# Bucket tiles of four heads stacked by transfers, and the maximum taken by four exponentials in every unit

## The reference

```python
q = split_heads(hidden_states @ Wq + bq)          # 16 heads of 8 features
k = split_heads(hidden_states @ Wk + bk)
scores = jnp.einsum('bhqd,bhkd->bhqk', q, k) / scale
pos_k = (rel_embeddings @ Wk + bk)                # 64 buckets of relative position
c2p_att = jnp.einsum('bhqd,hpd->bhqp', q, pos_k)
c2p = jnp.take_along_axis(c2p_att, c2p_pos, axis=-1)
p2c_att = jnp.einsum('bhkd,hpd->bhkp', k, pos_k)
p2c = jnp.swapaxes(jnp.take_along_axis(p2c_att, p2c_pos, axis=-1), -1, -2)
probs = jax.nn.softmax(scores + (c2p + p2c) / scale, axis=-1)
out = einsum('bhqk,bhkd->bhqd', probs, v) @ Wo + bo + hidden_states
out = layernorm(out, 1e-7) * ln_scale + ln_bias   # a second, plain layer norm follows
```

## Time and profile before

| what | value |
|---|---|
| median of 3 executions | 2843.77 us (2837.84 to 2845.44) |
| the profiled execution's own time | 2838.59 us |
| its span (first to last instruction) | 2836.9 us |
| busy in the span: TensorE, VectorE, ScalarE, GpSimd | 85%, 79%, 81%, 25% |
| mean granted TensorE clock | 0.939 of full |

### The profile page before, as it was taken

How to read it: one execution, slowest core, us unless ns; L and a number is a source line. 1 busy time by engine, 2 the same in 40 slices (tenths; PEclk the granted TensorE clock), 3 DMA queues, 4 the chain that set the end, 5 groups by cost and what they waited for, 6 DMA issues and landing times. The chain is left out here.

```text
span 2836.9 us, 64292 instructions
## 1 busy us (share of the span) xinstructions
PE 2414.7 (85%) x18180; PEld 1323.1 (47%) x18199; DVE 2232.0 (79%) x6591; ACT 2286.8 (81%) x4255; POOL 711.7 (25%) x565
## 2 busy tenths in 40 slices
PE   2888888888888337746699999999999999999997
PEld 1555555555555226614344444444444444444443
DVE  3788888788888576785488888888888888888887
ACT  1888888888888353317699999999999999999997
POOL 2334534544444101124311111111111111111114
PEclk7899999999999659977799999999999999999999
DMA  2000000000000100000011111211111121111113
GB/s 78 13 22 12 11 17 16 11 13 20 11 11 12 44 0 1 0 30 0 16 45 53 52 45 45 60 45 45 52 52 45 45 60 45 45 53 51 45 45 89
DMA packets 182540, 96.04 MB, mean 34 GB/s; under 512 B 22539, under 2 KB 179291, under 8 KB 182491
## 3 DMA queue, kind: packets, MB, share of 16 engines
q1 hardware_dynamic: 182491, 95.45, 12.0%
HBM read 78.10 MB, written 4.73 MB: 29 GB/s over the span
## 5 line engine op out<-in xcount | busy, mean ns | idle before, releaser
L1955 DVE TENSOR_TENSOR c_Hl<-c_HF,c_Hh 128x512 f16<-128x512 f32 x1028 | 679.6, 688 | 160.9 <-ACT c_Hh L1842 144.7
L1838 ACT ACTIVATE c_HF<-c_H,c_b 128x512 f32<-128x512 f32 x1028 | 711.0, 692 | 64.2 <-PE c_H L1777 44.3
L1842 ACT ACTIVATE c_Hh<-c_H,c_b 128x512 f16<-128x512 f32 x1028 | 706.4, 687 | 0.0
L1893 POOL TENSOR_TENSOR c_EX<-c_euler,c_D 128x16 f32<-128x16 f32 x65 | 188.6, 2902 | 1194.6 <-DVE c_D L1928 1194.6
L1775 PE MATMUL c_H<-c_Ch,SH 128*128 128x512 f16 x1028 | 390.1, 379 | 0.0
L1777 PE MATMUL c_H<-c_Ch,SH 128*128 128x512 f16 x1028 | 390.0, 379 | 0.0
L1776 PE MATMUL c_H<-c_Cl,SH 128*128 128x512 f16 x1028 | 390.0, 379 | 0.0
L1786 PE MATMUL c_Y<-c_Hh,SH 128*128 128x512 f16 x1024 | 388.1, 379 | 0.3 <-DVE c_Hl L1955 0.3
L1788 PE MATMUL c_Y<-c_Hl,SH 128*128 128x512 f16 x1024 | 388.1, 379 | 0.0
L1787 PE MATMUL c_Y<-c_Hh,SH 128*128 128x512 f16 x1024 | 388.1, 379 | 0.0
L692 DVE CUSTOM_DVE_ANT_0 a_T<-a_S,a_POS 128x128 f32<-128x128 f32 x1024 | 234.8, 285 | 48.0 <-PE a_S L436 41.0
(11 more groups left out here) (300 smaller groups left out, 4372.8 us busy)
## 6 DMA issues: line engine op xcount, KB each, us to landing
c_CWB<-c_rows SPq DMA_DIRECT2D x260, 256.0 KB, 4.1
a_QN<-a_QH SPq DMA_DIRECT2D x128, 32.0 KB, 1.9
a_KN<-a_KH SPq DMA_DIRECT2D x128, 32.0 KB, 1.8
out<-d_O SPq DMA_DIRECT2D x16, 256.0 KB, 2.3
a_QN<-a_QL SPq DMA_DIRECT2D x64, 32.0 KB, 1.9
a_KN<-a_KL SPq DMA_DIRECT2D x64, 32.0 KB, 1.8
CUR<-in_ctx SPq DMA_DIRECT2D x1, 1848.0 KB
c_rows<-c_CWR SPq DMA_DIRECT2D x65, 8.0 KB, 1.4
```

Source lines behind the costliest of these rows:

```text
L1838: act.activation(HF[:, k % 4, :], bH[k % 4][:, :], ACT.Gelu_apprx_tanh, bias=b1[:, g % EXPERTS, f:f + 1], scale=1.0 / WSCALE).then_inc(hf_ ...
L1842: act.activation(Hh[:, g % 2, f, :], bH[k % 4][:, :], ACT.Gelu_apprx_tanh, bias=b1[:, g % EXPERTS, f:f + 1], scale=1.0 / WSCALE).then_inc( ...
L1955: dve.tensor_tensor(Hl[:, g % 2, f, :], HF[:, k % 4, :], Hh[:, g % 2, f, :], ALU.subtract)\
```

## The change

- **Bucket tiles.** A tile now holds four heads in one copy (`TILES` 8). ScalarE writes the f16 high part without a scale to the new `ST`, VectorE the low part, and SyncE puts both into `AB` with 16 transfers of 128 KB a block (`stack_rows`), eight after the last query tile and eight after the last key tile. One tile a step, in steps 5 to 12. The first chunk waits for all 16. ScalarE's first write of each kind waits for the transfers of the block before.
- **Maximum.** `EARLY_MAX` is empty: `take_max` goes, and every unit has four exponentials.
- **Order.** The projections of queries, keys and values go to steps 1, 2 and 10 to 13; `high_half` goes behind the exponentials of steps 1 and 2, `low_half` to steps 2 and 3, `values_in` to 14. The last layer-norm step goes from step 9 to 14 and is written with a broadcast tensor in place of a second scalar. `QN` and `KN` have one semaphore a group.
- **Preparation.** The engines begin when the weights are in, and x comes in three transfers: the first four sequences, the next four, and the other 56 behind the small late loads. GpSimd's large fills come after its first copy. The table is half as wide, and VectorE's steps on it have half as many instructions.
- **TensorE.** Four 128x512 matmuls that nobody reads end the tail, ahead of the next block's scores. `V` has 16 columns a head, not 32.

```diff
-TILES = 4 * NG
+TILES = 2 * NG
-NORM_STEPS = (2, 3, 4, 5, 6, 7, 9)
+NORM_STEPS = (2, 3, 4, 5, 6, 7, 14)
+TILE_STEPS = (5, 6, 7, 8, 9, 10, 11, 12)
+V_STEPS = (10, 11, 12, 13)
-EARLY_MAX = range(6, 14)
-VCOLS = 32
+EARLY_MAX = range(0, 0)
+VCOLS, TILE = 16, 32
...
-        HM = sb("HM", [P, 2, TOK], F16)
-        AB = sb("AB", [P, S, 2, NG, 2, NB], F16)
+        ST = sb("ST", [P, 2, 2, S, NG, NB], F16)
+        AB = sb("AB", [P, 2, 2, S, NG * NB], F16)
...
+            def stack_rows(i, nxt, kind):
+                hold(sp, spare_sp, ab_ok.sem, ab_ok.at(i, TILES * nxt + (kind + 1) * NG))
+                if nxt:
+                    hold(sp, spare_sp, g_ps.sem, g_ps.at(i, CHUNKS))
+                for h in range(HG):
+                    for low in range(2):
+                        at = 64 * (h // 2) + 32 * low
+                        sp.dma_start(AB[at:at + 32, kind, h % 2, :, :].rearrange("p s x -> p (s x)"),
+                                     ST[32 * h:32 * h + 32, kind, low, :, :, :].rearrange("p s g b -> p (s g b)"))\
+                            .then_inc(ab_in[kind].sem, 16)
...
-                for src, dst in loads + late:
+                for src, dst in loads:
                     sp.dma_start(dst, src).then_inc(loaded, 16)
+                for n in range(2):
+                    sp.dma_start(X[:, n * NB:(n + 1) * NB, :], tokens[:, n * NB:(n + 1) * NB, :]).then_inc(x_in, 16)
+                    if n == 0:
+                        sp.wait_ge(x_in, 16)
+                for src, dst in late:
+                    sp.dma_start(dst, src).then_inc(late_in, 16)
             def body(i):
                 stack_queries(i, 1)
                 stack_keys(i, 1)
+                for kind in range(2):
+                    stack_rows(i, 1, kind)
...
             def position_chunk(i, nxt, c):
                 if c == 0:
-                    pe.wait_ge(ab_ok.sem, ab_ok.at(i, TILES * (1 + nxt)))
+                    for done in ab_in:
+                        pe.wait_ge(done.sem, done.at(i, done.per * (1 + nxt)))
...
-                                         AB[64 * f:64 * f + 64, at, :, :, :, :], start=True, stop=True)
+                                         AB[64 * f:64 * f + 64, :, :, at, :], start=True, stop=True)
...
+                    if u == UNITS + TAIL - 1 and not last:
+                        for _ in range(4):
+                            pe.matmul(bO[:, :], window[:, 0:P], table[:, 0:2, :, :].rearrange("p g k n -> p (g k n)"),
+                                      start=True, stop=True)
...
             def high_rows(i, nxt, n):
                 act.wait_ge(a_ps.sem, a_ps.at(i, TILES * nxt + n + 1))
-                act.wait_ge(ab_ok.sem, ab_ok.at(i, TILES * nxt + n - 1))
-                act.activation(HM[:, n % 2, :], bG[n % 2][:, :], ACT.Copy, scale=low_rows[:, :]).then_inc(hm_ok.sem, 1)
+                kind, g = n // NG, n % NG
+                if g == 0 and nxt:
+                    act.wait_ge(ab_in[kind].sem, ab_in[kind].at(i, ab_in[kind].per))
+                act.activation(ST[:, kind, 0, :, g, :], bG[n % 2][:, :].rearrange("p (s b) -> p s b", b=NB),
+                               ACT.Copy).then_inc(hm_ok.sem, 1)
...
             def split_rows(i, nxt, n):
-                dve.tensor_tensor(AB[:, :, kind, g, j, :], bG[n % 2][:, :].rearrange("p (s b) -> p s b", b=NB),
-                                  HM[:, n % 2, :].rearrange("p (s b) -> p s b", b=NB), ALU.subtract)\
-                    .then_inc(ab_ok.sem, 1)
+                dve.tensor_tensor(ST[:, kind, 1, :, g, :], bG[n % 2][:, :].rearrange("p (s b) -> p s b", b=NB),
+                                  ST[:, kind, 0, :, g, :], ALU.subtract).then_inc(ab_ok.sem, 1)
...
-                    last = dve.tensor_scalar(X[:, bass.ds(i * NB + b, 1), :], R[:, b, :], mv[:, b, 0:1],
-                                             rstd[:, b:b + 1], ALU.subtract, ALU.mult)
+                    last = dve.scalar_tensor_tensor(
+                        X[:, bass.ds(i * NB + b, 1), :].rearrange("p a h -> p (a h)"), R[:, b, :], mv[:, b, 0:1],
+                        rstd[:, b:b + 1].to_broadcast([P, H]), ALU.subtract, ALU.mult)
```

More of the change, by code:

```diff
@@ L58, in by_dve, with tiles_of @@
     return sum(1 for k, f in DVE_CHUNKS if k <= c)
+def tiles_of(u):
+    return [n for n, step in enumerate(TILE_STEPS) if step == u]
 def row_x(kind, g, j, b):
-    return ((kind * NG + g) * 2 + j) * NB + b
+    return ((kind * 2 + j) * NG + g) * NB + b
 class Count:
@@ L268, in body @@
                 stack_keys(i, 1)
+                for kind in range(2):
+                    stack_rows(i, 1, kind)
             stack_queries(0, 0)
             stack_keys(0, 0)
+            for kind in range(2):
+                stack_rows(0, 0, kind)
             body(0)
@@ L356, in body @@
             def body(i, first=False, last=False):
+                if first:
+                    pool.wait_ge(x_in, 32)
+                    pool.wait_ge(late_in, LATE)
                 if not last:
                     copy_block(i, 1)
-                if not first:
-                    power(i - 1, 0)
                 for u in range(UNITS):
@@ L363, in body @@
                         take_max(i, u)
-                    if u == NORM_STEPS[5] and not first:
-                        power(i - 1, 1)
-                residuals(i)
+                    if u in (NORM_STEPS[1], NORM_STEPS[5]) and not first:
+                        power(i - 1, (NORM_STEPS[1], NORM_STEPS[5]).index(u))
+                residuals(i, first)
                 if not last:
@@ L500, in _ @@
             pe.wait_ge(tab, 5)
-            project_qk(0, 0)
-            project_v(0, 0)
+            project_q(0, 0)
+            project_k()
+            for b in range(NB):
+                project_v(b)
             pe.wait_ge(tab, TAB)
@@ L527, in body @@
                     if u == 1 and not last:
-                        project_qk(i, 1)
+                        project_q(i, 1)
                     if u == 2 and not last:
-                        project_v(i, 1)
-                    for n in range(2 * (u - 6), 2 * (u - 6) + 2):
-                        if 0 <= n < TILES and not last:
+                        project_k()
+                    if u in V_STEPS and not last:
+                        project_v(V_STEPS.index(u))
+                    for n in tiles_of(u):
+                        if not last:
                             bucket_tile(i, 1, n)
@@ L861, in body @@
                             softmax_outputs(i, b)
-                    if u == 1 and not last:
-                        low_half(i, 1, 0)
-                        low_half(i, 1, 1)
-                    if u == 2 and not last:
+                    if u in (2, 3) and not last:
+                        low_half(i, 1, u - 2)
+                    if u == 14 and not last:
                         values_in(i, 1)
@@ L868, in body @@
                         norm_step(i - 1, NORM_STEPS.index(u))
-                    for k in range(2 * (u - 6), 2 * (u - 6) + 2):
-                        if 0 <= k < TILES and not last:
+                    for k in tiles_of(u):
+                        if not last:
                             split_rows(i, 1, k)
```

146 lines of the change are left out of this document (75 added, 71 removed).

## The result

The changed kernel takes 2735.16 us (median of 4 runs, 2734.89 to 2737.46), the kernel before 2844.47 beside it (2837.84 to 2845.44): a ratio of 0.9622, interval 0.9606 to 0.9639, or 109 us less. The profiled execution took 2735.33, with a span of 2733.6. The forecast of 2733 is 2 us off.

The account below looks back on a forecast made before the run. The prediction took ScalarE and its waits as the bound, then the transfers. Blocks (91.5 us) and preparation (19.5) off the profiled 2838.6 gave 2727.6; with 5.2 for the median, 2733, its own range 2708 to 2758.

Parts of the forecast that it names:

- The block: Attention block: head 35.8 us, ended by the transfers, plus tail 12.8 make 48.6 for 54.7, a gain of 6.1.
- a sign of being wrong: Head of the block: SyncE's queue, now with 40 transfers a block, would itself be what ends the head.
- rival 2: ScalarE's ST copies are written at xT's slow rate: 4.0 us a block, 60 in all, 2793 us; chance 0.07.
- Rival 3: Stacking transfers are slower than the queue issues them: 2.4 us a block, 2774 us in all; chance 0.08.
- The first reading of the profile: Steps with bucket tiles, before: ScalarE busy 20.55 of 22.60 us and VectorE less, so ScalarE is the engine to count.
- ScalarE's sum: Head: ScalarE's operations add to 33.9 us after the change and 34.0 before, so only waits can be won.
- ScalarE's waits: Head: 0.6 us of VectorE's 1.8 stays and step 14 costs 0.3, so ScalarE's head is 34.8.
- GpSimd's 2.6 go with `take_max`: Head: ScalarE's waits for GpSimd's subtraction, 2.6 us a block, vanish when the subtraction is removed.
- The preparation: Before the first chunk: start 15.9 us earlier, table work 4.1 less, first chunk at 53.2 for 72.70, 19.5 won.
- Rival 4: GpSimd holds up the norm step in step 14: 2.1 us a block for 0.3, 2760 us in all; chance 0.10.
- Rival 5: Transfers make the kernel slower: from 1.55 us each the whole gain is gone, at 2.0 it takes 2898; chance 0.04.
- Rival 1: Half the head's waits stay, 4 us instead of 0.9: a block wins 3.0, 2779 us in all; chance 0.12.

Follow-up runs that it names:

- e10: Changed kernel with each of a block's last eight stacking transfers cut into two of half the bytes: 2837.82 us, ratio 0.9986 to before.
- e4: Changed kernel with the last norm step moved back from step 14 to step 9, in its new form: 2740.72 us, ratio 0.9652 to before.
- e2: Kernel before with GpSimd's subtraction taken out (`EARLY_MAX` empty) and nothing else: 2844.19 us, ratio 1.0011 to before.
- e5: Changed kernel with GpSimd's subtraction back in units 6 to 13 and the last norm step in step 9: 2758.27 us, ratio 0.9713 to before.
- e11: Changed kernel with its bucket tiles two a step, in steps 5, 7, 9 and 11: 2752.48 us, ratio 0.9684 to before.
- e7: Changed kernel with TensorE, ScalarE and VectorE waiting at their start for all loads again: 2758.47 us, ratio 0.9715 to before.
- e1: Changed kernel with GpSimd's subtraction back in units 6 to 13, last norm step still in step 14: 2837.63 us, ratio 0.9985 to before.
- e6: Changed kernel with GpSimd's subtraction back and the last norm step in step 14 in its old form: 2837.66 us, ratio 0.9988 to before.
- e3: Changed kernel without the four idle matmuls at the end of the tail: 2743.30 us, ratio 0.9655 to before.
- e8: Changed kernel with the last norm step in step 9 and GpSimd issuing four of the eight last transfers: 2732.32 us, ratio 0.9623 to before.
- e9: Changed kernel with GpSimd issuing four of the eight last transfers, `values_in` at step 13, norm step in 14: 2730.74 us, ratio 0.9607 to before.

## Why the prediction was right, point by point

**The block, 48.6 forecast, 48.72 measured.** The head is 36.24 for 35.8, the tail 12.48 for 12.8, and the mean of 13 blocks fell by 5.9 for 6.1. The attention ends (SyncE's first load of the next stage) at 844.77 for 950.26, so 105.5 of the forecast 111 us are there. Of the rest 1.7 is missing in the preparation, 3.3 in the 14 blocks of the loop (82.1 for 85.4) and 0.5 in the first and the last block, which gained 2.9 and 2.7 for the 6.1 given to the two. What ends the head is, as forecast, the transfers, with 0.58 us of wait for the 1.0 given. After `scores(0)` the last eight are issued from 29.4 to 33.7 us and are in at 36.2, for a forecast of 29.2, 33.6 and 35.8. e10 shows that it is the number of issues (0.6 each) and not the bytes, and e4 that a last tile 0.22 late is paid there one for one. It is SyncE's queue that ends the head, which I had called a sign of being wrong, but by these eight issues alone: the queue of 40 had run empty at 26.9 and waited for the last tile. The price of an ST copy (0.48 forecast, 0.47 in the row) held, and the tail is 0.3 shorter than forecast; rival 2 is refuted by the 597 ns. Rival 3 is refuted by the queue's row (16 issues in 12.44 us, 0.78 each with the wait for the last tile in them) and the landing of 2.4.

**The total, in part luck.** The sum gave 2727.6 for the profiled execution, and that one took 2735.3, 7.7 more: 5.5 us short in the attention, 2.2 in the program behind it (1888.8 us from SyncE's first load for 1886.6). The 5.2 that I added, because the median of before lay that far above its profiled execution, had nothing to stand for in the changed kernel, whose median is 2735.16 beside a profiled 2735.33. It made up for most of the shortfall.

**The first reading of the profile was wrong.** In the steps with tiles 20.55 of 22.60 us are VectorE's busy time, and ScalarE's are 19.22; I had put the 20.55 down to ScalarE. ScalarE's sum does not use the number, and in the changed kernel ScalarE is the busier one (19.46 for 16.14), so the forecast came to no harm. But the kernel before was less ScalarE's than I said: e2 could give ScalarE 5.3 us more a block there at no cost.

**ScalarE's waits, mis-sized but hidden.** I kept 0.6 of VectorE's waits and 0.3 for step 14; measured are 1.8 a block (24.9 over 14), 0.79 of it in front of unit 15. ScalarE would have been ready at about 35.7 by that, still not after the transfers, so the sum didn't suffer.

**"GpSimd's 2.6 go with `take_max`": the step that fell, as an attribution.** I took 2.6 of the gain to be these named waits. e2 takes the subtraction from the kernel before and wins nothing in time: 5.6 us of waits go, not 2.6, and 5.3 of exponentials come. e5 has it back in the new arrangement and loses 1.1 a block. So of the 5.9 a block, 4.6 come with the subtraction still there (54.62 to 50.05, which includes the four idle matmuls' 0.3), and 1.1 to 1.35 with its removal. Of the 4.6, e11 gives 1.3 to the spacing of the tiles, if it is worth as much with the subtraction there; that was not run. The remaining 3, half of the block's gain (eight copies fewer, the value projections out of the block's start, VectorE's fewer instructions), I did not separate. The block's total came out because work and waits were both counted: five us of copies go, five of exponentials come, the waits fall from 7.9 to about 2.3.

**The preparation, 19.5 forecast, 17.8 measured.** From the first transfer of queries to the first chunk 27.3 us were measured for 27.0. The term that was mis-sized is the start: VectorE begins at 9.93 as forecast (10.2), but its table is 9.66 behind instead of 8.2, in part since its instructions stretch beside GpSimd's fills, which the change put there; e7 shows 8.36 with the fills out of the way. That the start's shift passes through is shown by e7 too.

**Rival 4, no collision, by 0.15 us.** It had a chance of 0.10 and a price of 27 us. The runs show the mechanism to be real and its price to be three times that: 4.7 us in step 14 and 1.9 in the tail, 79 us between e1 and e5. I had priced one GpSimd instruction of 2.1 us in between; in e1 three VectorE instructions of 0.34 in a row each wait one out. And it doesn't come with the new form, as I had written: e6 has the old one and the same time. The Trainium skill ("SBUF — State Buffer", Who interferes with whom, a part of SBUF: two separate sides) names more than the two inputs: `tensor_scalar` can enter a two-port mode in which it contends with GpSimd, and whichever issues first has the shared ports for the whole instruction. My prediction used only the half on two inputs. The durations agree, each long one ending about 0.15 us behind a GpSimd instruction; no run shows the mode. That the changed kernel is spared was not foreseen but isn't chance from block to block either: the 0.15 us is the same in every block of it and of e3, e7, e10 and e11. TensorE's last scores release GpSimd, which then passes its waits on semaphores, nearly 1 us, before the spreading starts. Six of those waits came with the change (one semaphore a group, about 0.1 us each); whether the norm step would be hit without them was not run.

**Rival 5, the other side,** needed 1.55 us a transfer; the landing row and the queue's refute it. Rival 1 is refuted by the head of 36.24, with 2.3 us of waits left in it.

## What to carry to other kernels

A wait in an engine's name is not what its removal brings: price the work that comes in its place, and try each half of a change alone in both kernels, since the same edit (the subtraction) was worth 0, 1.1 and 7 us a block depending on what stood beside it. When SBUF-to-SBUF work of VectorE and long instructions of GpSimd can meet, look up by how much they miss each other: here a step cleared GpSimd by 0.15 us, and cost 79 in the run in which another edit had made GpSimd late. And a stall on TensorE costs more than itself if it is long enough for its clock to fall: count the stretch behind it too.

## What the runs showed of the hardware

- A wait of TensorE of about 5 us was followed by some 7 us at a mean granted clock of 0.66 to 0.67, part of them at 1.2 GHz and the rest at 2.4: +1.8 us of tail in e10, +1.9 in e1 (means of 13 blocks). The wait of 0.58 in the changed kernel cost no clock.
- Four matmuls of 1.04 us together, in a wait of TensorE, kept the clock at 1.00 at the start of each block but the first; without them every third one started at 0.66 and took 0.8 to 1.4 us longer.
- VectorE's instructions from SBUF to SBUF of 0.34 us lasted 1.37, 2.20 and 2.16 beside GpSimd instructions of 1.38, 2.03 and 2.12 (e1), each to 0.15 us behind the end of GpSimd's. One input or two made no difference (5.77 and 5.83 for four).
- A transfer from 32 rows to 32 rows of SBUF lands 2.4 us after issue at 128 KB, 2.0 at 64 KB and 1.9 at 32 KB from SyncE; at 128 KB from GpSimd's queue it takes 3.6. Where GpSimd had issued transfers, the change to the next stage took 5.56 us for 1.57 (e8, e9).
- ScalarE's write in pieces of 8 bytes at a pitch of 32 took 597 ns, as the contiguous one of the same size (0.58).
